# Two blocks' scatters issued one at a time, and the maxima of the last block transposed ahead of an output step

## The reference

```
x = x + xattn(layernorm(x), ctx)          # q = n @ Wq.T + bq, softmax(q k / sqrt(32)) v, @ Wo.T + bo
n = layernorm(x)
w = softmax(n @ W_router.T + b_router)    # the two largest are kept, the others set to zero
x = x + sum_e w[e] * (n @ W_e.T + b_e)
```

## Time and profile before

| | |
|---|---|
| timed runs, median (lowest to highest) | 1269.87 us (1268.43 to 1270.14) |
| the profiled execution | 1271.68 us |
| its span, first to last instruction | 1270.0 us |
| TensorE busy | 1192.7 us, 94% |
| VectorE, ScalarE, GpSimd busy | 69%, 56%, 59% |
| mean granted TensorE clock | 0.977 of full |
| chain that ended last: TensorE, DMA, waits for nothing shown | 21%, 7%, 4% |

### The profile page before, as it was taken

One profiled execution on the slowest core, in us unless ns is written; L12 is line 12 of the kernel. 1 busy time (PEld: TensorE's weight loads), 2 busy tenths in 40 slices (PEclk: granted clock), 3 DMA queues, 4 the chain that ended last, 5 costly groups with the idle time before them and its releaser, 6 DMA issues. The chain is left out here.

```text
span 1270.0 us, 35737 instructions
## 1 busy us (share of the span) xinstructions
PE 1192.7 (94%) x11024; PEld 719.1 (57%) x11025; DVE 873.1 (69%) x1933; ACT 717.4 (56%) x1040; POOL 745.0 (59%) x980
## 2 busy tenths in 40 slices
PE   7977999999999999999999988689899999999997
PEld 4444666666666666666666654444455555555554
DVE  3666798889888888988987876445455555555554
ACT  4327757966976786697687547233333333343333
POOL 4004337767866866776786578655645454554445
PEclk9979999999999999999999989789999999999999
DMA  9754535855765675586557448868999999898886
GB/s 249 223 166 119 142 127 159 245 168 188 229 197 191 197 223 184 173 255 181 194 170 219 153 140 303 312 151 206 200 178 177 176 189 180 168 183 165 159 165 127
DMA packets 135544, 239.19 MB, mean 188 GB/s; under 512 B 18439, under 2 KB 49415, under 8 KB 134279
## 3 DMA queue, kind: packets, MB, share of 16 engines
q1 hardware_dynamic: 102503, 161.24, 43.0%
q0 software_dynamic: 29808, 67.73, 26.4%
q10 hardware_dynamic: 3120, 8.68, 2.0%
HBM read 112.00 MB, written 101.40 MB: 168 GB/s over the span
## 5 line engine op out<-in xcount | busy, mean ns | idle before, releaser
L1902 PE MATMUL S<-we_s,wq_s 128*128 x1620 | 375.3, 382 | 13.2 <-DVE wq_s L1858 5.6
L1830 POOL DMA_INDIRECT out<-xn,to x135 | 208.8, 1547 | 209.4 <-DMA out<-xn,to 135.6
L1902 PEld LDWEIGHTS S<-we_s,wq_s 128*128 128x128 f16 x1620 | 157.6, 98 | 180.7 <-issue 21.8
L1170 POOL TENSOR_TENSOR we_s<-P_s,we_s 128x1024 f16<-128x1024 f32 x96 | 204.7, 2134 | 93.6 <-ACT we_s L936 92.8
L1841 ACT ACTIVATE wq_s<-PVp 128x512 f16<-128x512 f32 x137 | 81.6, 597 | 269.2 <-PE PVp L1892 243.7
L984 DVE TENSOR_REDUCE mx_sb<-S 128x6 f32<-128x924 f32 x160 | 171.4, 1112 | 11.9 <-PE S L726 8.9
L1880 DVE SCALAR_TENSOR_TENSOR att<-S,be_s 128x512 f32<-128x512 f32 x135 | 93.4, 692 | 108.8 <-PE S L1902 100.6
L746 PE MATMUL W<-wo_s,aT_hi 128*128 128x512 f16 x512 | 164.8, 384 | 3.0 <-issue 1.7
L708 PE MATMUL W<-we_s,wq_s 128*128 128x512 f16 x512 | 160.0, 384 | 4.4 <-DVE xnT_lo L962 3.6
L1858 DVE TENSOR_TENSOR wq_s<-PVp,wq_s 128x512 f16<-128x512 f32 x137 | 94.6, 691 | 39.1 <-ACT wq_s L1841 32.4
L818 PE MATMUL PVp<-Vm,we_s 128*128 128x33 f16 x3072 | 118.7, 178 | 0.2
(11 more groups left out here) (208 smaller groups left out, 2000.5 us busy)
## 6 DMA issues: line engine op xcount, KB each, us to landing
P_s<-dispatched SPq DMA_DIRECT2D x139, 260.5 KB
we_s<-we_s SPq DMA_DIRECT2D x186, 128.0 KB
be_s<-in_x SPq DMA_DIRECT2D x16, 1024.0 KB
xR_s<-in_x SPq DMA_DIRECT2D x16, 1024.0 KB, 8.1
out<-xR_s SPq DMA_DIRECT2D x16, 1024.0 KB
wst<-in_weT SPq DMA_DIRECT2D x16, 512.0 KB, 5.4
we_scratch<-wsp SPq DMA_DIRECT2D x16, 512.0 KB
Kst<-k_scratch SPq DMA_DIRECT2D x16, 480.0 KB, 10.0
```

Of the source, the lines that this page charges most:

```text
L1170: e.tensor_tensor(Pst[1][:, r:r + 2, :], exps(n), Pst[0][:, r:r + 2, :], ALU.subtract).then_inc(pldp, 1)
L1830: e.indirect_dma_start(out, bass.IndirectOffsetOnAxis(ap=to[u][:, :], axis=0), yw[u % YW], None, bounds_check=N - 1, oob_is_err=False, com ...
L1902: m = e.matmul(Yp[:, u % 2, :], gT[u % 2][xp][:, k, :], we_s[:, bass.ds(n * WN + (wp * KC + k) * D, D)], start=(c == 0), stop=(c == 11))
```

## The change

Two edits. In `pool_slot` the condition for single scatters is widened from blocks up to 11 to blocks up to 13, and the calls of the grouped ones go. Block 12 then issues four scatters in the slot function 13 and four in 14, block 13 four in 14 and four in 15. In `pe_slot` output step 11 stays where it was as long as there is a block s+2; in slots 14 and 15 it comes after product 5 of block s and, in slot 14, after the transpose of the maxima of block 15 (in slot 15 there are no maxima left).

```diff
--- before.py
+++ after.py
@@ -1467,12 +1467,14 @@
             pe_O(e, bm1, 10, s)
         if on_bp1:
             pe_MX(e, bp1, 10, s)
-        if on_bm1 and not bm1.last:
+        if on_bp2 and on_bm1:
             pe_O(e, bm1, 11, s)
         if on_b:
             pe_PV(e, b, 5)
         if on_bp1:
             pe_MT(e, bp1, s)
+        if not on_bp2 and on_bm1 and not bm1.last:
+            pe_O(e, bm1, 11, s)
         lb = bm1 if on_bm1 and not bm1.last else None
@@ -1665,10 +1667,10 @@
-        early1, early2 = on_bm1 and bm1.here(EARLY - 2), on_bm2 and bm2.here(EARLY - 2)
+        singles1, singles2 = on_bm1 and bm1.here(NB - 3), on_bm2 and bm2.here(NB - 3)
         if on_bp1:
             pool_PL(e, bp1, 2)
-        if early2:
+        if singles2:
             pool_S1(e, bm2, 4)
...
         if on_bp1:
             pool_PL(e, bp1, 7)
-        if early1:
+        if singles1:
             pool_S1(e, bm1, 0)
         if on_bp1:
             pool_PL(e, bp1, 8)
-        if early1:
+        if singles1:
             pool_S1(e, bm1, 1)
-        elif on_bm1 and bm1.here(NB - 3):
-            pool_SC(e, bm1)
         if on_b:
             pool_BX(e, b, 3)
-        if early1:
+        if singles1:
             pool_S1(e, bm1, 2)
         if on_b and not b.last:
             pool_NC(e, b, 1)
             pool_RQ(e, b)
-        if early1:
+        if singles1:
             pool_S1(e, bm1, 3)
-        elif on_bm1 and bm1.here(NB - 3):
-            pool_SD(e, bm1)
         if on_bp2:
             pool_PL(e, bp2, 0)
```

## The result

The changed kernel took 1274.17 us in the median of 20 runs (1268.2 to 1280.3), the kernel before, run beside it, 1269.54 us (20 runs, 1264.64 to 1275.91). The ratio is 1.003, with a 95% interval of 1.0016 to 1.0044: slower by some 3.8 us (2.0 to 5.6; the medians lie 4.6 apart). The forecast was 1.2 us more than before, 1271.1 us, so the sign of the sum was right and its size was too small by 2.6 us; the most likely case, "within 0.2%", is not where the ratio lies, though the lower end of its interval does.

The account below looks back on a forecast made before the run. The prediction took GpSimd's queue at the end of slot 15 as the bound. Its only nonzero term in the sum was +1.2 us there: 1269.9 + 1.2 = 1271.1 us, forecast's own range 1269.5 to 1273.0, full range 1266.9 to 1274.4.

Parts of the forecast that it names:

- within 0.2%: Whole kernel: time within 2.5 us of the median before, chance 0.70; 0.10 below that and 0.20 above.
- Single scatters in slot 15: GpSimd, slot 15: six single scatters (7.24 us) replace a group (5.55 us), so the bias addition ends 1.21 us later.
- the thinned group of slot 14: GpSimd, slot 14: three scatters go, pair 0's subtraction can start at about 768 instead of 771.75; worth 0.
- the stall goes with the group: Faster rival: the wait until 772.8 us disappears, GpSimd's queue runs 2.6 us earlier; -1.4 us, 1268.5; chance 0.24.
- from the bias addition on everything hangs in series: After slot 15's bias addition: evacuation through router logits and block 15's transposes follow in series, so 1.21 us pass on.
- Slots 16 and 17: GpSimd: block 14's group of eight ends 3.8 us later, but idle time before the second add takes that up.
- Absorbed: Rival: the 1.2 us vanish in TensorE's unexplained waits ahead of the second expert tile; 1269.9 us; chance 0.12.
- Product 4 held: TensorE, slot 15: block 15's product 4 waits 4.2 us for pair 7's subtraction, replacing the 4.84 us wait; costs nothing.
- Clock: Slower rival: low clock behind the new gap, five pieces take at most twice their time; 1274.4 us; chance 0.18.
- The transpose: TensorE, slot 14: block 15's maxima transposed 0.54 us earlier, VectorE's evacuation 1.5 us later; 0 in the sum.
- The stall at 772.8: ScalarE and VectorE waits of 2.60 and 1.81 us that no row explains; the forecast keeps them where they are.
- Block 14's group slides under the first expert tiles: Rival: unexplained TensorE waits follow the scatters and last longer by 3.8 us; 1273.7 us; chance 0.06.

Follow-up runs that it names:

- a2: Kernel before with only the single scatters (conditions in `pool_slot`), TensorE's order unchanged: 1261.39 us, ratio 0.9988.
- c4: a2 run again in the third set, single scatters without the edit of TensorE's order: 1264.0 us, ratio 1.001.
- c3: Kernel before, with block 15's pair 0 subtraction moved ahead of block 12's second group, TensorE's order unchanged: 1263.1 us, ratio 1.0006.
- b1: a3 with the six single scatters ahead of block 14's last bias addition issued behind it, in slot function 14: 1268.25 us, ratio 0.9999.
- b2: a2 with the six single scatters ahead of block 14's last bias addition issued behind it, in slot function 14: 1267.94 us, ratio 0.9991.
- b4: Kernel before, with block 13's first group of four scatters issued behind block 14's last bias addition: 1269.28 us, ratio 1.0003.
- a4: The changed kernel once more, unaltered: 1267.16 us (9 runs), ratio 1.0046 against the kernel before.
- a1: Kernel before with only the changed places of output step 11 in slots 14 and 15, scatters as before: 1263.62 us, ratio 1.0017.
- c2: Kernel before with the edit of TensorE's order, and block 15's pair 0 subtraction ahead of block 12's second group: 1263.68 us, ratio 1.0014.
- a3: Changed kernel plus one GpSimd wait, holding block 15's pair 0 subtraction until block 13's logits are done: 1261.9 us, ratio 1.0001.
- c1: a2 with only block 13's scatters 0 and 1 issued behind block 14's last bias addition: 1261.58 us, ratio 1.0001.
- b3: Changed kernel, with block 12's scatter 4 between GpSimd's subtractions of pairs 0 and 2 in slot function 14: 1271.73 us, ratio 1.0021.

## Why the prediction was right or wrong

**Single scatters in slot 15 (forecast +1.21 us).** Close for this stretch, and wrong for the path. From pair 3's subtraction to the bias addition the prediction's prices give five scatters, 1.23 + 2.53 + 1.16 + 1.16 = 6.08 us, for the group's 5.55: +0.53. Measured: 798.05 - 778.24 = 19.81 us before, 798.25 - 777.75 = 20.50 after, +0.69. But where the single scatters stand alone (a2, c4), the bias addition came at t + 35.7, 1.4 us sooner than in the kernel before and not 1.2 later, because pair 3's subtraction had come 2.1 us sooner, at t + 15.17 instead of t + 17.26. GpSimd's rows of the kernel before and of a2:

```profile
778.24 2.13 POOL L1170 TENSOR_TENSOR we_s<-P_s,we_s 128x1024 f16<-128x1024 f32 x1
...
776.65 2.14 POOL L1170 TENSOR_TENSOR we_s<-P_s,we_s 128x1024 f16<-128x1024 f32 x1
```

(t is 760.98 and 761.48.) So the thinned group of slot 14, put down as "Worth 0, unless the stall below goes with it", was worth 2.1 us there, with the stall gone; at the addition 1.4 us sooner is just what the rival "the stall goes with the group" had forecast. The stall's end alone doesn't do it: c3 has none and keeps the group, and its subtraction of pair 3 starts at t + 17.48. The sign of the whole sum was therefore luck: its one term of +1.2 us is not what made the kernel slower. The step from the addition to the end, "from the bias addition on everything hangs in series, so 1.21 us pass on", holds to the first expert tile in all profiles but b1, b2 and b4, within the 1.3 us by which the last part of the way varies (see the table of b1 and b2). Whether it holds to the end of the kernel is not shown: the ratios of a2 and c4, 0.9988 and 1.001, don't tell -2.5, 0 and +1.2 us apart.

**Slots 16 and 17 (forecast 0).** Right where the single scatters stand alone: in a2 block 14's group of eight ended 1.1 us later than before (t + 72.0 against t + 71.0), and the first add came 0.6 us sooner. "Absorbed" did not come: the first expert tile of the changed kernel is 4.4 us later.

**Product 4 held (forecast 4.2 us).** Measured 2.84 us in the changed kernel, 3.16 in a4, 2.62 in c4. The mechanism was right, the gap smaller, and for different reasons. In c4 the subtraction of pair 7 ended at t + 31.2 and not at t + 33.9, for the reason told under the single scatters. In the changed kernel it ended at t + 37.1, 3.3 us later than forecast, but the output steps in front of the gap ended 4.6 us later.

**Clock (the slower rival, 0.18).** It took place in small. Behind the gap the granted clock fell (0.72 over 793 to 799, and 0.50 over 795 to 797, where matmuls of L746 stand 0.43 us apart instead of 0.216): the low level, which the prediction had named as a sign of being wrong. TensorE and not the addition ended the evacuation's wait, and its start at 799.99 is 0.46 us behind the addition's end at 799.53. The 4.5 us of the rival were bounded at twice all five pieces; the clock came back after 797.8 and spared the rest of them.

**The transpose (forecast 0.54 us earlier).** Right: from the start of the last reduction (L989) to t it took 1.53 us before and 1.01 after, and 1.00 or 1.01 in all seven profiles with the edit. VectorE's side was right as well. Pair 1's subtraction was to start at 769.1 with t 0.54 us earlier, which is t + 8.66; a1 measured t + 8.68. But the edit alone gave 1.0017 [1.0003, 1.0031] and not nothing (c2 and c3, 1.0014 and 1.0006, can't be told apart). So of the two bounds, -0.54 and +1.5 us, the taken 0 was too favourable. The path that was missing is GpSimd's: its router constants wait for VectorE's evacuation, so in a1 the group of four started at t + 8.06 instead of t + 5.88, pair 3's subtraction 1.5 us later (t + 18.74) and the last evacuation 2.7 us later (t + 41.19). That is one profile, seen and not tested by a run of its own.

**Where it failed.** The prediction did follow the logits: "all move 1.5 us". And it followed the subtraction: "pair 0's subtraction can start at about 768 rather than at 771.75. ... Worth 0". The delay of VectorE was right. The subtraction came at t + 9.00 and not at t + 7.0 (768 less 760.98), because the router constants in front of it on GpSimd hang on VectorE's later evacuation too (the last of them ends at t + 7.4 in the changed kernel, t + 5.3 before). But what failed is that an earlier subtraction was costed at zero or a gain. It was never asked what runs on VectorE at that moment, and the two shifts, counted from t 2.2 us later on the one engine (the logits, t + 5.95 to t + 8.12) and 1.8 us earlier on the other, brought together two operations that had been 4.2 us apart (the logits ended at 767.56, the subtraction began at 771.75). None of the rivals had it. The price was 4.76 us at VectorE (pair 1's subtraction at t + 13.43 and not at t + 8.67), seen in both profiles of the changed kernel, and a3 takes it all back. The upper end of the stated range, 1274.4 us, came from the clock's rival, so that the measured median lies just under it says nothing for the mechanism.

**Why 3.8 us and not 4.8 or 6.9.** The seam of the changed kernel is 6.9 us longer than a3's (114.32 and 107.43), and the kernel 5.3 us slower. Against the kernel before the seam is 3.8 us longer: the single scatters shorten it. In the first and third set a2 and c4 have 107.8 us where the grouped a1, c2 and c3 have 110.4, 109.7 and 110.9. That is the gain of 2 to 3 us that the rival "the stall goes with the group" had named, by GpSimd's queue being free sooner. It is not seen in the ratios. From the first expert tile to the end of the span a1 and c2 took 433.7 and 434.0 us, a2 and c4 437.2 and 439.5, but c3, with the group, took 436.8, and c1, with the shortest seam, 435.9. TensorE's waits from 820 to 900 us, in a1 and then in c4 (us in total, times, longest):

```profile
PE S L1904 <- DVE wq_s L1860: 3.8, 5, 2.0
...
PE S L1898 <- DVE wq_s L1854: 5.7, 2, 5.0
PE PVp L1888 <- DMA P_s<-dispatched: 1.8, 1, 1.8
```

and the granted clock from 850 to 860 us was 1.00 in a1 and c2, 0.83 in a2, c4 and c3. These rows suggest that an earlier start of the experts runs into rows of tokens that are not loaded yet. That is not shown: c3 started late and has the low clock too, c2 started late and has a wait for loads of 1.7 us, a1's profiled execution was the fastest of its twelve, 5.0 us under their median (c2's 2.8 under), and none of the runs changed the loads. Why the shorter seam brings no faster kernel stays open.

**The stall at 772.8 (kept).** It is gone in the changed kernel, as the faster rival had it, and any gain from that is hidden there by the lock. Whether it went with the group is left open by the runs. None of the eight profiles of the first and third set has any "remote" wait, with the group (a1, c2, c3) or without, so there the group didn't bring it. In the first comparison and on the chip of b1 to b4, where every profile has "remote" waits somewhere, it stands at t + 11.9 in the two kernels that keep block 12's second group, the kernel before and b4, and in none of the four without (the changed kernel, b1, b2, b3). The group alone is not enough, then; it may be part of the cause. "Block 14's group slides under the first expert tiles" came close in the number (1273.7), but not by its reason: the pieces of waiting among the first expert tiles did grow, as below (the changed kernel), but a4 is slower by no less and has no such pieces there.

```profile
832.86 0.59 PE L1900 MATMUL S<-we_s,wq_s 128*128 x1 [1.95 <-issue]
834.29 0.58 PE L1900 MATMUL S<-we_s,wq_s 128*128 x1 [0.84 <-issue]
835.70 0.59 PE L1900 MATMUL S<-we_s,wq_s 128*128 x1 [0.83 <-issue]
```

## What to carry to other kernels

When a change moves one of VectorE and GpSimd against the other, list for the new moment which operations of both read two tensors in SBUF: a 128x1 addition waited out a 128x1024 one, and a 128x8 operation two of them back to back. Such a wait stands in no wait table; it shows as a duration, so compare the longest with the median by source line. A step that "comes earlier and is worth 0" is still a change of who runs beside whom; and a bound found at one wait (GpSimd's addition) says nothing of the total until something has been moved out from in front of it.

## What the runs showed of the hardware

- VectorE's operation was held from before GpSimd's subtraction started in its row. In the changed kernel the second logits operation starts at 764.90 us and would have ended by 765.12, during the scatter; the subtraction's row begins at 765.64, and the operation stayed through both subtractions. In a3 the same operations ran beside the same scatter at 0.63 us for four, with the subtraction kept waiting. So by these rows a subtraction whose input is ready takes the port while the indirect DMA in front of it is still being issued, at least 0.5 us ahead of its own row. In c3 one whose input wasn't ready did not.
- After a gap of about 3 us behind steady work TensorE's granted clock was at its low level for a few us, but not from the same moment: in the changed kernel the first three matmuls of L815 behind the gap (793.82) took their usual 0.35 us, in a4 (794.29) 0.51 us.
- Whether the traces have "remote" and "issue" waits beside rows of scatters differs from chip to chip with the kernel unchanged: the changed kernel has "remote" ones in its first profile and none in a4. On the chip of b1 to b4 and in the first comparison, where every profile has "remote" ones, the kernel before took 1269.04 and 1269.54 us; on the two others, where none has, 1262.31 and 1262.37. What they are stays open.
